# One opening stage for tables and first projections, with plain stacks and position ends as nine rows

## What is computed

```python
Q, K, V = heads(x @ Wq.T + bq), heads(x @ Wk.T + bk), heads(x @ Wv.T + bv)
pos_key   = (rel_emb @ Wpk.T + bpk).reshape(128, 16, 8)
pos_query = (rel_emb @ Wpq.T + bpq).reshape(128, 16, 8)
r = clip(j - i + 64, 0, 127)          # i: query, j: key
scores = scale * (Q_i . K_j + Q_i . pos_key[r] + K_j . pos_query[clip(i - j + 64, 0, 127)])
ctx = softmax(scores) @ V
```

## Time and profile before

| | before |
|---|---|
| median of 3 runs | 2112.41 us (2110.75 to 2112.5) |
| the profiled execution | 2112.18 us, of which the profile's span is 2110.4 |
| TensorE busy | 1724.6 us (82%) |
| VectorE busy | 1468.4 us (70%) |
| ScalarE busy | 1466.8 us (70%) |
| DMA | 419996 packets, 420.89 MB, mean 199 GB/s |

### The profile page before, as it was taken

The page is one execution under the profiler, slowest core; times in us unless marked ns, Lnnn a source line. Parts: engine busy times, 40 slices in busy tenths (PEclk is TensorE's granted clock), DMA queues, the critical chain, the costliest instruction groups (busy, mean ns, idle before and its releaser), DMA issues. The chain is left out here.

```text
span 2110.4 us, 44034 instructions
## 1 busy us (share of the span) xinstructions
PE 1724.6 (82%) x11670; PEld 1044.7 (50%) x11670; DVE 1468.4 (70%) x3508; ACT 1466.8 (70%) x2584; POOL 79.4 (4%) x102
## 2 busy tenths in 40 slices
PE   2316999999999999983861799999999994999998
PEld 1203555555555555552540465565556552545544
DVE  2635888888888888872983788888888882423422
ACT  2304888888888888881872799999999993223222
POOL 0000000000000000000540000000000000000000
PEclk9656999999999999996985899999999997999999
DMA  2966999998899999955687777777777763100100
GB/s 71 353 217 195 271 270 276 275 269 271 271 274 277 270 271 276 272 163 153 206 299 257 200 210 213 213 213 211 212 212 213 211 180 100 35 20 22 37 5 10
DMA packets 419996, 420.89 MB, mean 199 GB/s; under 512 B 36016, under 2 KB 325320, under 8 KB 419808
## 3 DMA queue, kind: packets, MB, share of 16 engines
q1 hardware_dynamic: 419936, 420.19, 67.1%
HBM read 232.47 MB, written 187.00 MB: 199 GB/s over the span
## 5 line engine op out<-in xcount | busy, mean ns | idle before, releaser
L817 ACT ACTIVATE a_prob<-bank,a_negmax 128x512 f32<-128x512 f32 x1024 | 734.6, 717 | 51.3 <-DVE a_negmax L749 49.6
L749 DVE TENSOR_REDUCE a_negmax<-bank 128x1 f32<-128x512 f32 x1024 | 699.5, 683 | 0.2 <-issue 0.2
L631 PE MATMUL bank<-a_ident,a_prob 128*128 128x128 f32 x4096 | 644.1, 280 | 60.1 <-ACT a_probt L824 50.8
L824 ACT COPY a_probt<-bank 128x512 f32<-128x512 f32 x1024 | 616.2, 602 | 87.4 <-PE bank L631 73.7
L631 PEld LDWEIGHTS bank<-a_ident,a_prob 128*128 128x128 f32 x4096 | 449.5, 141 | 181.9 <-issue 76.5
L741 DVE TENSOR_TENSOR bank<-bank,a_band 128x128 f32<-128x128 f32 (+3 forms) x1024 | 350.2, 342 | 80.1 <-PE bank L612 68.4
L610 PE MATMUL bank<-a_stks 65*128 65x192 bf16 (+7 forms) x1024 | 323.0, 316 | 10.5 <-ACT a_prob L817 10.2
L644 PE MATMUL bank<-a_probt,a_vs 128*32 128x512 f32 x2048 | 272.4, 606 | 15.0 <-ACT a_probt L824 15.0
L610 PEld LDWEIGHTS bank<-a_stks 65*128 65x128 bf16 (+1 forms) x1024 | 100.1, 98 | 231.8 <-ACT a_prob L817 202.4
L729 DVE COPY_PREDICATED bank<-a_mask,bank 128x128 f32<-128x128 uint32 (+1 forms) x512 | 139.4, 272 | 107.2 <-PE bank L616 107.1
L612 PE MATMUL bank<-a_stks 65*128 65x320 bf16 (+5 forms) x768 | 201.1, 262 | 0.0
(11 more groups left out here) (169 smaller groups left out, 1567.9 us busy)
## 6 DMA issues: line engine op xcount, KB each, us to landing
a_band<-shear_b SPq DMA_DIRECT2D x128, 512.0 KB, 4.4
shear_a<-a_keyside SPq DMA_DIRECT2D x128, 256.0 KB, 3.4
a_sheared<-shear_a SPq DMA_DIRECT2D x128, 256.0 KB, 4.4
shear_b<-a_corr SPq DMA_DIRECT2D x128, 256.0 KB, 4.4
shear_e<-a_corr SPq DMA_DIRECT2D x128, 256.0 KB, 2.3
a_band<-shear_e SPq DMA_DIRECT2D x128, 256.0 KB, 3.4
a_stks<-stack SPq DMA_DIRECT2D x128, 192.0 KB, 4.5
a_stks<-stack SPq DMA_DIRECT2D x128, 144.0 KB, 2.9
```

What stands on the lines that cost most here:

```text
L631: last = pe.transpose(turned_bank[k][:, n * 128:(n + 1) * 128], prob[h.slot % 2][:, n, k * 128:(k + 1) * 128], ident[:, :])
L749: v.tensor_reduce(negmax[h.slot % 2][:, n:n + 1], score[:, :], AX.X, ALU.max, negate=True).then_inc(maxed, 1)
L817: nc.scalar.activation(prob[h.slot % 2][:, n, :], score[:, :], ACT.Exp, bias=negmax[h.slot % 2][:, n:n + 1]).then_inc(exped, 1)
L824: nc.scalar.copy(probt[h.slot][:, k, :], turned_bank[k][:, :]).then_inc(copied, 1)
```

## The change

One stage, `opening_phase`, takes the place of the two. It loads x and the weights of queries and keys first, projects sequence 0, and then makes the position tables between the first batches. `stack0` is now `[B, 2, C, NTERM, T]`: keys once and queries once, with their own biases alone. What the position ends add to a score is made apart: `w_off` is a weight matrix for 4 x 16 = 64 rows (for each head, the query against the low and high end of the position keys, and the key against the low and high end of the position queries), TensorE multiplies it with x (`offset_product`), and ScalarE and VectorE split the 64x512 result in three bfloat16 parts, written to `offsets` in HBM. In `stks` these stand as nine more rows behind the old 65: three of query offsets against ones in the keys, and six of key offsets against ones in the queries (`RA`, `RB`, `RS`). `stks` has 74 rows and 3 arrays where it had 65 and 4. Constant rows, `consts` and the three extra rows of `table` are gone. The score products now contract 74 rows; `key_side` and `correction` use the first 65.

`stks`, `tabs` and `ident` are allocated around both stages, so `opening_phase` blanks them, and from b = 3 on loads the tables, the offsets and the first seven heads, queued among its own writes. The attention stage raises the semaphores of these loads by hand. `head_load` issues two DMAs (96 and 48 KB) where it issued one of 192 KB, and `offset_load` three where `consts_load` issued one. The first values are loaded behind the first shears. Middle parts are now cast by ScalarE, which VectorE did before. The loop over sequences in the opening is written out.

```diff
@@ names and arrays in memory @@
-R0 = SR + 3
 R1 = 2 * SR
 RF = 65
-KHI, KLO, QLO, QHI = range(4)
+RA, RB, RS = RF, RF + 3, RF + 9
+KS, QLO, QHI = range(3)
...
-        stack = {0: dram("stack0", [B, C, NTERM, 4, T], BF16), 1: dram("stack1", [B, C, NTERM, ARRAYS, T], BF16)}
-        consts = dram("consts", [H, R0 - SR, 4, T], BF16)
+        stack = {0: dram("stack0", [B, 2, C, NTERM, T], BF16), 1: dram("stack1", [B, C, NTERM, ARRAYS, T], BF16)}
+        offsets = dram("offsets", [B, H, 4, 3, T], BF16)
         values = dram("values", [NG, 128, GROUP * NT * VC], F32)
-        table = dram("table", [H, R0, 2 * REL], BF16)
+        table = dram("table", [H, SR, 2 * REL], BF16)
@@ the two old stages are removed; the new one, its queue @@
-        def tables_phase():
+        def opening_phase(stks, tabs, ident):
...
+                        def write_stack(b):
+                            sp.wait_ge(lo_set, BASE + b + 1)
+                            for first, n, q in TERM_RUNS:
+                                sp.dma_start(stack[0][b, 0, :, first:first + n, :].rearrange("c j t -> c (j t)"),
+                                             part[b % 2][:, 0, 0:n, :].rearrange("c j t -> c (j t)")).then_inc(stack_out[b], 16)
+                                same = bass.AP(part[b % 2][:, :, :, :].tensor, (3 + q) * T, [[6 * T, C], [0, n], [1, T]])
+                                sp.dma_start(stack[0][b, 1, :, first:first + n, :], same).then_inc(stack_out[b], 16)
+                        def write_offsets(b):
+                            sp.wait_ge(off_lo, BASE + b + 1)
+                            sp.dma_start(offsets[b].rearrange("h a k t -> a h (k t)"),
+                                         off_part[b % 2][:, :, :].rearrange("p k t -> p (k t)")).then_inc(off_out[b], 16)
+                        def write_table(j):
+                            rows = table[:, :, :].rearrange("h (c j) r -> h c j r", j=NTERM)[:, :, j, :]
+                            sp.dma_start(rows[:, :, 0:REL], dpart[Q_PART[j]][:, 0, :]).then_inc(table_out, 16)
+                            sp.dma_start(rows[:, :, REL:2 * REL], dpart[K_PART[j]][:, 1, :]).then_inc(table_out, 16)
+                        def first_head(j):
+                            rows = stack[0][0, :, bass.ts(j, DH)].rearrange("a c j t -> (c j) a t")
+                            sp.dma_start(stks[0:SR, j, KS:QLO + 1, :], rows).then_inc(first_in, 16)
+                            sp.dma_start(stks[0:SR, j, QHI, :], rows[:, 1, :]).then_inc(first_in, 16)
...
+                        load_x(0)
+                        for dst, src in ((wq, t["WqT"]), (wk, t["WkT"]), (bq, t["bq"]), (bk, t["bk"])):
+                            sp.dma_start(dst[:, :], src).then_inc(q_in, 16)
+                        for dst, src in ((wv, t["WvT"]), (bv, t["bv"].partition_broadcast(128))):
+                            sp.dma_start(dst[:, :], src).then_inc(v_in, 16)
+                        for dst, src in ((relt, t["relT"]), (wpk, t["WpkT"]), (wpq, t["WpqT"]), (bpk, t["bpk"]), (bpq, t["bpq"]),
+                                         (negblock, t["negblock"]), (ident, t["ident"])):
+                            sp.dma_start(dst[:, :], src).then_inc(pos_in, 16)
+                        load_x(1)
...
+                        ones_of = bass.AP(ones[:, :].tensor, 0, [[T, 3], [0, UNROLL[0]], [1, T]])
+                        for at, arr in ((RA, KS), (RB, QLO), (RB + 3, QHI)):
+                            sp.dma_start(stks[at:at + 3, :, arr, :], ones_of).then_inc(filled, 16)
+                        for b in range(B):
+                            write_values(b)
+                            if b + 2 < B:
+                                sp.wait_ge(off_mm, BASE + b + 1)
+                                load_x(b + 2)
+                            write_stack(b)
+                            if b > 0:
+                                write_offsets(b - 1)
+                            if b < 3:
+                                if b == 0:
+                                    sp.wait_ge(dsplit, BASE + 4)
+                                for j in (2 * b, 2 * b + 1):
+                                    write_table(j)
+                            if b == 3:
+                                sp.wait_ge(stack_out[0], BASE + 16 * N_STACK)
+                                sp.wait_ge(off_out[0], BASE + 16)
+                                sp.wait_ge(table_out, BASE + 16 * 2 * NTERM)
+                                for g in range(UNROLL[0] // GROUP):
+                                    own = slice(GROUP * g, GROUP * g + GROUP)
+                                    sp.dma_start(tabs[0:SR, own, :], table[own].rearrange("h r c -> r h c")).then_inc(first_in, 16)
+                                    for arr in (QLO, QHI):
+                                        sp.dma_start(stks[RA:RB, own, arr, :], offsets[0, own, arr - QLO].rearrange("h k t -> k h t")).then_inc(first_in, 16)
+                                    sp.dma_start(stks[RB:RS, own, KS, :], offsets[0, own, 2:4].rearrange("h a k t -> (a k) h t")).then_inc(first_in, 16)
+                            if b > 3:
+                                first_head(2 * (b - 4))
+                                if b < B - 1:
+                                    first_head(2 * (b - 4) + 1)
+                        write_offsets(B - 1)
+                        sp.wait_ge(filled, BASE + 16 * N_FILL)
+                        sp.wait_ge(first_in, BASE + 16 * (2 * LOAD_AHEAD[0] + 4 * (UNROLL[0] // GROUP)))
@@ the new stage, ScalarE @@
+                        for b in range(1, B):
+                            queries_keys(b)
+                            high(b)
+                            offset_high(b - 1)
+                            middle(b)
+                            offset_middle(b - 1)
+                        offset_high(B - 1)
+                        offset_middle(B - 1)
@@ the new stage, VectorE @@
+                        v.memset(zf[:, :], 0.0).then_inc(blank, 1)
+                        v.memset(ones[:, :], 1.0).then_inc(blank, 1)
+                        for i in range(2):
+                            v.memset(vt[i][:, :, :, DH:VC], 1.0).then_inc(blank, 1)
+                        v.memset(tabs[0:RF, :, :], 0.0).then_inc(blank, 1)
+                        for j in range(UNROLL[0]):
+                            v.memset(stks[0:RS, j, :, :], 0.0).then_inc(blank, 1)
+                        v.wait_ge(v_in, BASE + 32)
+                        values_set(0)
...
+                        for b in range(1, B):
+                            values_set(b)
+                            remainder(b)
+                            offset_remainder(b - 1)
+                            low(b)
+                            offset_low(b - 1)
+                        offset_remainder(B - 1)
+                        offset_low(B - 1)
@@ attention_phase @@
-                per_stk = 16 if rel else 64
+                per_stk = 32 if rel else 64
...
-                        sp.dma_start(stk[j][0:SR, :, :], stack[0][b, own].rearrange("c j a t -> (c j) a t")).then_inc(stk_in[j], 16)
+                        rows = stack[0][b, :, own].rearrange("a c j t -> (c j) a t")
+                        sp.dma_start(stk[j][0:SR, KS:QLO + 1, :], rows).then_inc(stk_in[j], 16)
+                        sp.dma_start(stk[j][0:SR, QHI, :], rows[:, 1, :]).then_inc(stk_in[j], 16)
...
-                    sp.dma_start(tabs[0:R0, h.slot:h.slot + GROUP, :], src).then_inc(tab_in[h.slot // GROUP], 16)
-
-                def consts_load(sp, h):
-
-                    src = consts[bass.ds(h.n % H, GROUP), :, QHI, :].rearrange("h r t -> r h t")
-                    sp.dma_start(stks[SR:R0, h.slot:h.slot + GROUP, QHI, :], src).then_inc(consts_in[h.slot // GROUP], 16)
+                    sp.dma_start(tabs[0:SR, h.slot:h.slot + GROUP, :], src).then_inc(tab_in[h.slot // GROUP], 16)
+                def offset_load(sp, h):
+                    src, own = offsets[h.n // H, bass.ds(h.n % H, GROUP)], slice(h.slot, h.slot + GROUP)
+                    event = offset_in[h.slot // GROUP]
+                    for arr in (QLO, QHI):
+                        sp.dma_start(stks[RA:RB, own, arr, :], src[:, arr - QLO].rearrange("h k t -> k h t")).then_inc(event, 16)
+                    sp.dma_start(stks[RB:RS, own, KS, :], src[:, 2:4].rearrange("h a k t -> (a k) h t")).then_inc(event, 16)
...
-                            consts_load(sp, Head(i, j + 5))
+                            offset_load(sp, Head(i, j + 5))
...
-                            sp.wait_ge(blank, BASE + 1)
-                            head_load(sp, Head(0, 0))
-                            sp.wait_ge(blank, BASE + 1 + unroll)
+                            for j in range(load_ahead):
+                                sp.sem_inc(stk_in[j], per_stk)
                             for g in range(unroll // GROUP):
-                                tab_load(sp, Head(0, GROUP * g))
```

(28 more changed lines are left out.)

392 lines of the change are left out of this document (185 added, 207 removed).

## The result

The kernel after took 2092.4 us (median of 4 runs, 2090.2 to 2093.7), the kernel before beside it 2111.7: ratio 0.991, 95% interval 0.990 to 0.992. It is faster by 19 us (0.9%) where 57 were forecast, and it lies outside the range. The profiled execution took 2092.2 us, span 2090.0. Each later ratio is against executions of the kernel before that were timed beside it. All figures are of fast executions; one execution of `before_head`, at 2917 us and a granted clock of 0.56, was slow and is left out.

The account below looks back on a forecast made before the run. It took the first projections as bound by bytes written to `stack0`, the steady heads as engines in balance, TensorE a little ahead. Gains of 54.7 + 1.5 + 1 = 57.2 from 2112.18 gave 2055.0 us, range 2040 to 2072.

Parts of the forecast that it names:

- Opening: One opening stage moves the attention's first keyside copy from 159.95 to 105.3 us, a gain of 54.7.
- the first stack write: Opening's first write to `stack0`, forecast at 21.5 us where it was 54.80.
- the boundary: Semaphore clears and increments between opening and attention: 100 operations, 7.0 us, ending at 101.9.
- the engines' share in the batches: In the opening, 72.0 us of work on four DMA engines over 1.03 is 69.9, so the stage ends at 94.9.
- Four engines: Opening's offsets' write runs on four engines, so 8.2 us a batch; rival with all 16: 2043 us, chance 0.17.
- opening slower than priced: Rival: 1 KB runs or the chain through two buffers hold an opening batch at 9.7 us; 2067 us, chance 0.15.
- Fill: Attention's pipeline filling, its first shears no longer sharing engines with six head loads: 1.5 us gained, bounds 0 and 4.
- Score products: Contraction in the attention's heads grows from 65 to 74 rows: priced at nothing; 10 ns each would cost 23 us.
- Steady heads: Attention's heads after the fill: a gain of 1 us, bounds 18 lost and 3 gained.
- Bands land sooner: In steady heads the DMA share falls to about 0.78 and band reads land sooner, paying for the later issue.
- One band in four is asked for 0.7 later: Extra SyncE issues in steady heads delay band reads; as rival up to 18 us lost, 2065 to 2073, chance 0.12.
- 0.5 is absorbed: VectorE has room in steady heads, so a late band costs only what exceeds about 0.5 us.

Follow-up runs that it names:

- before_head: Kernel before with its head load split in two DMAs of the same bytes, one more issue in each step; 2125.4 us.
- all_six: Kernel after: four x buffers, 64-row offsets' write, offset loads over two steps, second head load behind sheared read, three buffers for stacks' and offsets' parts; 2048.3 us.
- off_sixteen: Kernel after with offset rows ordered by head, so that the offsets' write has an outermost dimension of 64 in place of 4; 2079.0 us.
- x_four: Kernel after with four buffers for x in place of two; 2086.0 us.
- both_opening: Kernel after with four x buffers and the offsets' write on 64 outer rows together; 2079.9 us.
- before_read_last: Kernel before with the sheared read put behind the group's store and values load in the group's last step, no issue added; 2153.8 us.
- read_first: Kernel after with the sheared read put ahead of the step's head, table and offset loads, the same issues; 2063.5 us.
- before_three: Kernel before with the group's load of constant rows split in three DMAs by heads (1, 1 and 2), the same bytes; 2130.4 us.
- before_issues: Kernel before with the head load split in two and the constants' load in three single rows, the same bytes; 2211.0 us.

## Why the prediction was wrong

**Opening, 54.7 forecast, 47.3 measured.** The first DMA (4.41 for 4.0), the first stack write (22.17 for 21.5), the boundary (103.0 to 110.3, 7.3 for 7.0) and the hand-over to the first copy (2.4 for 3.4) held. The term that was mis-sized is the engines' share in the batches: I divided the four engines' 72.0 us by 1.03. The work was priced right: 0.78 of 16 engines for 74 us is 924 us; seven offset writes at 7.6 are 53 of it, so by this estimate each of the four had 871/16 + 53/4 = 67.7 us in 74, a share of 0.92, and with the 5 us behind it they come to about the 72.0. 72.0 over 0.92 is 78.3, 8.4 more than 69.9; the stage ended at 103.0 instead of 94.9. The old batches kept 1.01. Here a batch waits in turn for the four engines and for buffers, and without the narrow write and with more buffers (all_six) the share was still 0.91, so the four engines are not the whole reason.

**Four engines.** No offsets write has a landing time, the end runs at 0.25 of the engines, and off_sixteen, whose write has a landing time, gave 10.5 us. By the rule of the Trainium skill that the prediction cites ("DMA: Bandwidth & Descriptors", section "Why a DMA increments its semaphore by 16 and not by 1"), a write with an outermost 4 runs on four engines; this trace agrees, with a share of 0.25 at 97 GB/s from 102 to 103 us.

**Batch chain.** The rival "opening slower than priced" named 1 KB runs and the buffer loop; x_four says the loop for x is worth at most 1.7 us while the four engines hold, which is within what the copy moves by itself, and both_opening 3.1 us once they don't.

**Fill.** 2.2 for 1.5, a difference smaller than the copy's own movement. **Score products.** Priced at nothing, and so they came out. In after they take 397 ns for 512 columns against 389 at 65 rows, at a granted clock of 0.99 in 300 to 800 us; in all_six, with the same 74 rows and a clock of 1.00, they take 389:

```profile
L690 PE MATMUL bank<-a_stks 74*128 74x512 bf16 x81 | 32.1, 397 | 0.0
```

```profile
L703 PE MATMUL bank<-a_stks 74*128 74x512 bf16 x84 | 32.7, 389 | 0.0
```

**Steady heads, a gain of 1 forecast, 29.8 lost.** This is the step that failed, in three parts. "Bands land sooner": I had the DMA share fall from 0.91 to 0.78, since I set the old head loads at 20 us of engine time a head, read from the 6 us stretch at 153 us. It fell to 0.86. By size, the 10,342 packets of 4 KB of the kernel after in 300 to 800 us, all band reads, took 250 ns in the mean and 159 in the median; before had 14,803 at 224.5, 10,752 of them for its 84 bands. If its band packets took 250 too, the head loads' took 157 ns, 7.5 us a head: my 7.3, not 20. A stretch at the fill was no measure of the steady heads. The 13 us of engine time a head that my price left over lie in the band reads, whose 128 packets took 250 ns each where the price gives about 150. "One band in four is asked for 0.7 later": this nearly held (0.5 and 0.6 in the two tables). But the landing was held fixed in the sum, and in one of the two heads it grew by 1.4: the slack that SyncE lost had kept the sheared read, the store and the values out of that band's way. "0.5 is absorbed" is the third part: in the other head, where the landing did not change, the band came 0.6 later and VectorE waited 0.7 longer for it. Of 2.8 us of longer band waits in eight heads its waits for TensorE gave back 0.8, which is 0.4 for each of the two late bands.

**What stays open.** That the order of the queue brings the late landing is shown by before_read_last and read_first; how, is argued only. While such a band is in flight the engines are about 0.9 busy in either case (0.92 in before, 0.87 in after, for the heads of the first table), so it probably shares them with more of what was asked for ahead of it. But in those heads the landing falls at once from 5.8 to 4.2 between 3.14 and 3.42 us ahead. And the heads 2 more than a multiple of 8 land after 5.4 us in before already, with the read 3.16 ahead, and still after 4.85 in read_first, with 5.25. No run explains these steps, nor the long packets of the band reads.

## What to carry to other kernels

Before adding DMA issues to a queue whose engine has idle time, look at what that idle time separates: a transfer that a compute engine waits for can land later when the ones ahead of it move up to it, even if it is asked for at the same moment (before_head and before_three). Put new loads behind the transfers of the critical loop, not ahead of them; moving one line gave 25 to 29 us here. And when a DMA's outermost dimension is small, price it on that many engines, and do not assume that any engines stay full while batches wait for buffers.

## Not expected of the hardware

Putting one DMA behind two others in SyncE's program, with the same bytes and count, made the kernel 2.0% slower (before_read_last). Three one-row DMAs took SyncE 2.2 us (before_issues), where three of three rows took 1.15 (before_three). Reading 128 rows of 4 KB at a pitch one element short of their own costs no more than at their own (share 0.86 against 0.87, landing 4.3 against 4.4 us).
